# Graph attention: fetch each edge's row once in the maxima walk, store the rows in edge order, load them plainly in the sums walk, and weigh them on GpSimd

## The chip, the cores and the metric

One core of a Trainium2 chip runs a four-layer network (three graph layers of different kinds, and feed-forward parts between them) as one program. The metric is the device time of one execution in microseconds, the median of several. Engines are named as in the profile: PE (matrix), DVE (vector), ACT (scalar), POOL (GpSimd), SP (the engine that here only issues transfers).

## The reference, cut to what matters

Only the graph attention of the second layer is touched. It has 3125 nodes with 256 features (4 heads of 64) and 53125 edges, sorted by destination.

```
h = (x @ W).reshape(N, H, C)
a_s = jnp.einsum('nhc,hc->nh', h, att_src)
a_d = jnp.einsum('nhc,hc->nh', h, att_dst)
e = a_s[src] + a_d[dst]
e = jnp.where(e > 0, e, NEG_SLOPE * e)
m = jax.ops.segment_max(e, dst, num_segments=N)
p = jnp.exp(e - m[dst])
denom = jax.ops.segment_sum(p, dst, num_segments=N)
alpha = p / (denom[dst] + 1e-16)
msg = h[src] * alpha[:, :, None]
agg = jax.ops.segment_sum(msg, dst, num_segments=N)
```

The kernel first finds each destination's greatest `a_s` over its edges (the leaky step is monotonic, so the greatest `e` follows from it), and then sums weighted rows and weights, and divides at the end.

## The kernel before, in words

`graph_attention` (line 1495) has these stages in a row, each ended by a barrier of all engines.

**Rows and scores** (lines 1505 to 1580). PE makes `h` for 25 tiles of 128 nodes. Each row of 256 features and its 4 source scores goes to a table in DRAM, `table_gat` (rows of 260 floats), by one store per tile (line 1527). At the end the 4 source scores alone go to a second table, `table_max` (rows of 4 floats), by one store (line 1529).

**The maxima walk** (lines 1583 to 1690). The edges lie in 440 columns of 128 slots, taken in 110 quads of Q = 4 columns. Nothing here is scheduled by a planner: `written_out` writes out, for each engine, the steps of a turn in the order in which they are listed, each so many quads ahead. For each column POOL issues one gather of 128 rows (line 1625) from `table_max` into a ring of 8 quads; ACT makes diagonal matrices of three heads (line 1606) and a mask (line 1609), DVE those of the first head (line 1662) and the one-hot matrix of destinations (helper at line 126), PE spreads the scores over destinations (lines 1642 and 1644), and DVE takes the maxima (line 1673) and keeps them (line 1684).

**The sums walk** (lines 1693 to 1845), over the same 110 quads. POOL gathers 440 times 128 rows of 260 floats from `table_gat` (line 1737) into a ring of 8 quads in the tile `wide`. PE turns the one-hot matrix (line 1751), fetches each edge's destination scores by it (line 1760), and multiplies the one-hot matrix by the weighted rows (line 1768) into four banks, one for each column of a quad. ACT copies the turned matrix (line 1717) and takes the exponential (line 1722). DVE's turn for quad j is, in this order: one-hot of j+4 (line 126), weights times rows of j+1 (line 1828, 128x1024) with a copy of the weights behind them (line 1829), and then by turns the four additions of bank s to the node sums (line 1839) and the four small steps of the exponent of j+2 (lines 1809, 1812, 1816, 1821):

```
            mixed = [f for n in range(4) for f in ((0, add(n)), (2, exponents(n)))]
            written_out(R, (4, hots), (1, weigh), *mixed)
```

PE's turn is `(2, scores), (0, sums), (4, turn_hots)`. The product of bank s for the next quad waits until bank s has been added (`pe.wait_ge(added, j * Q + s + 1)`), an addition waits for the one before it, and a gather into a ring place waits until the sums of eight quads before are done. POOL has nothing but gathers in both walks; SP has one transfer at the start of the sums walk (line 1710, the nodes' own rows). Between that transfer and the walk DVE weighs the nodes' own rows (line 1792).

Of the kernel before, what the change touches and what calls it, by code (L numbers as in the profile page):

```python
# [16 lines left out]
ALU = mybir.AluOpType  # L17
# [161 lines left out]
def setup_memory(nc, ctx):  # L179
    class M:  # L180
        pass

    m = M()

    def sb(name, shape, dt=F32):
        return ctx.enter_context(nc.sbuf_tensor(name, shape, dt))

    m.X = sb("residual", [P, NT, D])
    m.XN = sb("normed", [P, NT, D])
    m.XT = sb("normed_T", [P, KD, NP])  # L190
    m.AGG = sb("sums", [P, NT, AW])
    m.BB = sb("wide", [P, 2 * NT * D])
    m.WS = sb("work", [P, 7168])
    m.PS = ctx.enter_context(nc.psum_tensor("ps", [P, 8, 512], F32))
    m.ident = sb("ident", [P, P])
    m.identb = sb("identb", [P, P], BF16)
    m.iota = sb("iota", [P, P])
    m.upto = sb("upto", [P, P])
    m.before = sb("before", [P, P])
    m.binsel = sb("binsel", [P, 2 * NT - 1], BF16)  # L200
    m.x_loaded, m.rec_blanked, m.rows_blanked = (
        nc.alloc_semaphore(s) for s in ("x_loaded", "rec_blanked", "rows_blanked"))
    m.ones = sb("ones", [P, P])
    m.zerob = sb("zerob", [P, 160], BF16)
    m.real = sb("real", [P, NT])
    m.wiota = sb("wiota", [NT, WP])
    m.coef = sb("coef", [P, KD, 2])
    m.gate = sb("gate", [P, NT, 8])

    m.lo1 = sb("lo1", [P, WP])  # L210
    m.src1 = sb("src1", [P, WP], I32)
    m.rel1 = sb("rel1", [P, WP], I32)
    m.tn1 = sb("tn1", [1, WP], I32)
    m.tn2 = sb("tn2", [1, WP], I32)
    m.lo_e, m.oth_e = sb("lo_e", [P, ET]), sb("oth_e", [P, ET])
    edges = m.XN[:].rearrange("p t d -> p (t d)")
    m.slot, m.type_e, m.col_e, m.row_e, m.lo_d, m.oth_d = (edges[:, k * ET:(k + 1) * ET] for k in range(6))
    m.record = sb("record", [P, ET], I32)
    m.forth, m.back = sb("forth", [P, 2, NT], I32), sb("back", [P, 2, NT], I32)
    m.expert = sb("expert", [1, 64], I32)  # L220
    m.onesb = sb("onesb", [P, P], BF16)
    m.notafterb = sb("notafterb", [P, P], BF16)
    m.beforeb = sb("beforeb", [P, P], BF16)
    m.iotah = sb("iotah", [P, WP], F16)
    m.zerow = sb("zerow", [P, WP + 1], BF16)
    m.AF = m.AGG[:].rearrange("p t d -> p (t d)")
    m.keys = [edges[:, k * ET:(k + 1) * ET].bitcast(I32) for k in range(6, 9)]
    m.keys_loaded = nc.alloc_semaphore("keys_loaded")
    m.blank = view(m.WS, 4352, BLANK // 4, EA + 4)
    m.zeros = view(m.WS, 5632, 6 * D)  # L230
    m.rec2 = nc.dram_tensor("rec2", (P * WP, EA + 4), F32).ap()
    m.rows_in = nc.dram_tensor("rows_in", (ROWS + 2 * P, D), F32).ap()
    m.rows_out = nc.dram_tensor("rows_out", (ROWS, D), F32).ap()
    m.table = nc.dram_tensor("table", (NP, D), F32).ap()
    m.table_gat = nc.dram_tensor("table_gat", (NP, D + 4), F32).ap()
    m.table_max = nc.dram_tensor("table_max", (NP, 4), F32).ap()
    m.table_rel = nc.dram_tensor("table_rel", (8 * NP, D), F32).ap()
    return m

# [1255 lines left out]
def graph_attention(nc, m, a):  # L1495
# [7 lines left out]


    with Stage(nc) as st:
        (loaded, made, copied, weighed, scored, rowed, bulked, tabled) = (
            st.sem(s) for s in ("loaded", "made", "copied", "weighed", "scored", "rowed", "bulked", "tabled"))
        stored = st.sems("stored", U)
        BANKS = 8
        row = view(m.WS, 0, U, RW)  # L1510
# [8 lines left out]
        def _(sp):  # L1519
# [5 lines left out]
            for t in range(NT):  # L1525
                sp.wait_ge(rowed, t + 1)
                sp.dma_start(to[:, t, :], row[:, t % U, :]).then_inc(stored[t % U], 16)
            sp.wait_ge(bulked, 1)
            sp.dma_start(m.table_max.rearrange("(t p) c -> p t c", p=P), src_score).then_inc(tabled, 16)
            for s in range(U):  # L1530
                sp.wait_ge(stored[s], 16 * (NT // U))
            sp.wait_ge(tabled, 16)

        @block.scalar
        def _(act):
# [24 lines left out]
        def _(dve):  # L1560
# [16 lines left out]
                             ).then_inc(scored, 1)  # L1577
            dve.wait_ge(scored, NT)
            v.tensor_copy(node[:, :, 0:H], scores[:, :, H:2 * H])
            v.tensor_copy(src_score, scores[:, :, 0:H]).then_inc(bulked, 1)  # L1580


    with Stage(nc) as st:
        names = ("hot", "masked", "made", "topped", "bested", "initial")
        hot, masked, made, topped, bested, initial = (st.sem(s) for s in names)
        R, RS = 8, 4
        gathered = st.sems("gathered", R * Q)
        S = view(m.WS, 0, RS * Q, P)
        off = view(m.WS, RS * Q * P, RS * Q * P // 2).bitcast(BF16).rearrange("p (u e) -> p u e", e=P)
        o = RS * Q * P * 3 // 2  # L1590
        rows = view(m.WS, o, R * Q, H)
        top = view(m.WS, o + R * Q * (H + 1), 2 * Q, H)
        minus = m.WS[:, o + R * Q * (2 * H + 1):o + R * Q * (2 * H + 1) + 1]
        diag = high[:, 0:RS * Q * H * P].rearrange("p (u h e) -> p u h e", u=RS * Q, h=H)
        MASK = float(2.0 ** 100)
        block = st.block()

        @block.scalar
        def _(act):
            def masks(j, u, r):  # L1600
                k = u % RS
                act.wait_ge(made, j + 1 + R - RS)
                for s in range(Q):
                    act.wait_ge(gathered[u * Q + s], r * 16 + 16)
                    for h in range(1, H):
                        nc.scalar.mul(diag[:, k * Q + s, h, :], m.ident[:], rows[:, u * Q + s, h:h + 1])  # L1606
                act.wait_ge(hot, j + 1)

                nc.scalar.activation(off[:, k * Q:(k + 1) * Q, :], S[:, k * Q:(k + 1) * Q, :], ACT.Identity,  # L1609
                                     bias=minus, scale=MASK).then_inc(masked, 1)  # L1610

            act.wait_ge(initial, 2)
            written_out(R, (2, masks))

        @block.gpsimd
        def _(pool):
# [1 line left out]
            nc.gpsimd.tensor_copy(best, src_score).then_inc(initial, 1)  # L1618

            def gather(j, u, r):  # L1620
                if j >= R:
                    pool.wait_ge(made, j + 1)
                for s in range(Q):
                    q, w = u * Q + s, j * Q + s
                    nc.gpsimd.indirect_dma_start(rows[:, q, :], None, m.table_max,  # L1625
                                                 bass.IndirectOffsetOnAxis(ap=m.src1[:, w:w + 1], axis=0)
                                                 ).then_inc(gathered[q], 16)

# [22 lines left out]
        def _(dve):  # L1651
# [3 lines left out]
            dve.wait_ge(initial, 2)  # L1655

            def first_heads(j, u, r):
                k = slice(u % RS * Q, (u % RS + 1) * Q)
                dve.wait_ge(made, j + 1 + R - RS)
                for s in range(Q):  # L1660
                    dve.wait_ge(gathered[u * Q + s], r * 16 + 16)
                v.tensor_tensor(diag[:, k, 0, :], m.ident[:].unsqueeze(1).to_broadcast([P, Q, P]),
                                rows[:, u * Q:(u + 1) * Q, 0:1].to_broadcast([P, Q, P]), ALU.mult)

            def hots(j, u, r):
                k = slice(u % RS * Q, (u % RS + 1) * Q)
# [26 lines left out]
    with Stage(nc) as st:  # L1693
# [2 lines left out]
        (dstep, ready, own_diffed, own_expd, selfed, hot, turned, tcopied, scored, taken, estep, diffed,  # L1696
         expd, weighted, summed, added) = (st.sem(s) for s in names)
        R, RT = 8, 4
        gathered = st.sems("gathered", R * Q)
        S = view(m.WS, 0, R * Q, P)  # L1700
        ST = view(m.WS, R * Q * P, RT * Q, P)
        o = (R + RT) * Q * P
# [5 lines left out]
        @block.sync  # L1708
        def _(sp):
            sp.dma_start(m.AGG[:, :, 0:RW], m.table_gat.rearrange("(t p) c -> p t c", p=P)).then_inc(selfed, 16)  # L1710

        @block.scalar
        def _(act):
# [15 lines left out]

        @block.gpsimd  # L1730
        def _(pool):
            def gather(j, u, r):
                if j >= R:
                    pool.wait_ge(summed, (j + 1) * Q)
                for s in range(Q):
                    q, w = u * Q + s, j * Q + s
                    nc.gpsimd.indirect_dma_start(rows[:, q, :], None, m.table_gat,  # L1737
                                                 bass.IndirectOffsetOnAxis(ap=m.src1[:, w:w + 1], axis=0)
                                                 ).then_inc(gathered[q], 16)

            written_out(R, (0, gather))

        @block.tensor
        def _(pe):
# [32 lines left out]
        def _(dve):  # L1777
# [22 lines left out]
            def exponents(n):  # L1800

                def step(j, u, r):
                    k = slice(u * Q, (u + 1) * Q)
                    sc = m.PS[:, 2 + u % 2, 0:Q * 8].rearrange("p (s c) -> p s c", s=Q)
                    if n == 0:
                        for s in range(Q):
                            dve.wait_ge(gathered[u * Q + s], r * 16 + 16)
                        dve.wait_ge(scored, j + 1)
                        v.tensor_tensor(e[:, k], rows[:, k, D:RW], sc[:, :, 0:H], ALU.add).then_inc(estep, 1)
                    if n == 1:  # L1810
# [10 lines left out]
                        v.tensor_scalar(e[:, k], e[:, k], 0.0, None, ALU.min).then_inc(diffed, 1)  # L1821
                return step

            def weigh(j, u, r):
                k = slice(u * Q, (u + 1) * Q)
                dve.wait_ge(expd, j + 1)
                f = rows[:, k, 0:D].rearrange("p s (h c) -> p s h c", h=H)
                v.tensor_tensor(f, f, p[:, k].unsqueeze(3).to_broadcast([P, Q, H, C]), ALU.mult)
                v.tensor_copy(rows[:, k, D:RW], p[:, k]).then_inc(weighted, 1)

            def add(s):

                def step(j, u, r):
# [8 lines left out]

            node_tile, tiles = NodeTiles(nc, dve, m.tn1), [None] * Q
            mixed = [f for n in range(4) for f in ((0, add(n)), (2, exponents(n)))]
            written_out(R, (4, hots), (1, weigh), *mixed)


    with Stage(nc) as st:
# [1318 lines left out]
```

## Time and profile before

| | us |
|---|---|
| median of three runs | 6393.75 |
| the three runs | 6400.41, 6391.69, 6393.75 |
| span of the profiled execution | 6396.8 |
| busy: PE, DVE, POOL, ACT | 4980.4, 3277.9, 3406.6, 1623.8 |

The profile gives no time for the profiled execution beside its span. Its span stands 3.05 us above the median of the runs. Busy shares are averages over some forty stages with different limits, so the two walks are read by themselves, from the lines, waits and timeline of their stretches. In a row of the timeline the first number is the start, the second the duration of that instruction or of a merged run of equal ones (`x4`); two instructions of one engine overlap by a little where they are pipelined.

### The profile page before, as it was taken

The numbers are of one execution on the slowest core, as the hardware profiler recorded it, in microseconds if no ns is written. First come the engines' busy times: TensorE is split into PE (matmuls) and PEld (weight loads), VectorE is DVE, ScalarE is ACT, GpSimd is POOL, SyncE is SP. The second block draws the span as 40 slices with busy tenths as digits, with TensorE's granted clock in tenths as the row PEclk, the third lists the DMA queues.
The fourth block names the chain that finished last, engine by engine and source line by source line (L and its number), as shares of the span: only waits on it lengthen the run. The fifth ranks groups of instructions, "written<-read, shape, count | busy, mean of one in ns | idle before, by whom it ended". The sixth has DMA issues, their size and how long they took to land. (4 is left out here: it accounts for less than half of the span.)

```text
span 6396.8 us, 72731 instructions
## 1 busy us (share of the span) xinstructions
PE 4980.4 (78%) x20184; PEld 3081.3 (48%) x20185; DVE 3277.9 (51%) x7777; ACT 1623.8 (25%) x3879; POOL 3406.6 (53%) x3602
## 2 busy tenths in 40 slices
PE   7968877887676888788863997799988568888455
PEld 2233334333445333355652886688875333343244
DVE  8954444444456777776772112566656332444412
ACT  4920002000323888511111221233331111000111
POOL 3147774777151777777735655467730211777223
PEclk7979998999788999888876998899999779999777
DMA  5023342334111000233323774333330334333255
GB/s 198 5 77 104 103 100 74 104 103 102 29 34 25 2 2 2 58 97 97 97 46 120 226 218 150 95 114 115 114 73 2 114 102 135 103 104 103 38 177 175
DMA packets 405943, 597.93 MB, mean 93 GB/s; under 512 B 131551, under 2 KB 305952, under 8 KB 405472
## 3 DMA queue, kind: packets, MB, share of 16 engines
q0 software_dynamic: 144992, 337.62, 20.1%
q1 hardware_dynamic: 257392, 252.99, 12.9%
q8 instruction: 151, 2.47, 0.2%
q10 hardware_dynamic: 3216, 3.28, 0.2%
q14 instruction: 192, 1.57, 0.1%
HBM read 472.47 MB, written 121.17 MB: 93 GB/s over the span
## 5 line engine op out<-in xcount | busy, mean ns | idle before, releaser
L784 PE MATMUL ps<-wide 128*128 128x256 f32 x2640 | 915.5, 429 | 323.0 <-DMA wide<-table,src 188.6
L811 DVE TENSOR_TENSOR sums<-sums,ps 128x256 f32 x1320 | 555.2, 421 | 981.8 <-PE ps L784 979.0
L769 POOL DMA_INDIRECT wide<-table,src x880 | 852.6, 969 | 276.5 <-PE ps L784 203.2
L784 PEld LDWEIGHTS ps<-wide 128*128 128x128 f32 x2640 | 407.3, 190 | 844.3 <-DMA wide<-table,src 557.6
L781 PE MATMUL ps<-zerow,zerob 128*128 128x440 bf16 x2640 | 713.4, 352 | 28.2 <-DVE wide L126 28.2
L769 POOL DMA_INDIRECT wide<-table_rel,rel x440 | 428.7, 974 | 351.5 <-ACTq L95 217.8
L1737 POOL DMA_INDIRECT wide<-table_gat,src x440 | 477.0, 1084 | 148.1 <-issue 122.8
L2379 POOL DMA_INDIRECT work<-table,work x440 | 451.8, 1027 | 187.8 <-issue 107.2
L1625 POOL DMA_INDIRECT work<-table_max,src x440 | 452.4, 1028 | 134.3 <-issue 134.3
L1644 PE MATMUL ps<-wide,work 128*128 128x512 f32 x880 | 451.1, 594 | 0.0
L1606 ACT ACTIVATE wide<-ident,work 128x128 f32<-128x128 f32 x1320 | 416.2, 388 | 64.9 <-DMA work<-table_max,src 61.1
L1768 PE MATMUL ps<-wide,work 128*128 128x260 f32 x880 | 332.3, 507 | 92.3 <-DVE sums L1839 92.0
L781 PEld LDWEIGHTS ps<-zerow,zerob 128*128 128x128 bf16 x2640 | 260.1, 99 | 223.5 <-DVE wide L126 29.9
L554 POOL DMA_INDIRECT rec<-sums,record x256 | 248.6, 971 | 176.0 <-DMA sums<-in_edge_attr 101.7
L719 ACT COPY work<-sums 128x256 f32<-128x256 f32 x100 | 33.1, 402 | 1203.1 <-PEq L723 1202.7
L1768 PEld LDWEIGHTS ps<-wide,work 128*128 128x128 f32 x880 | 178.4, 233 | 191.8 <-DVE sums L1839 162.9
L1673 DVE TENSOR_REDUCE work<-ps 128x16 f32<-128x2048 f32 x110 | 251.6, 2288 | 30.1 <-issue 27.3
L1642 PE MATMUL ps<-identb,work 128*128 128x512 bf16 x440 | 168.4, 383 | 125.9 <-ACT work L1609 125.9
L2407 PE MATMUL ps<-wide 128*128 x880 | 263.3, 381 | 1.1 <-DVE work L2445 1.1
L2408 PE MATMUL ps<-work,wide 128*128 128x256 f32 x880 | 262.7, 380 | 0.0
L701 PE MATMUL ps<-ident,normed 128*128 128x128 f32 x400 | 95.4, 425 | 199.7 <-DVE normed L647 199.3
L462 ACT ACTIVATE wide<-iotah,wide 128x441 f16<-128x441 f16 x416 | 230.3, 679 | 34.0 <-DVE wide L483 34.0
(474 smaller groups left out, 9031.7 us busy)
## 6 DMA issues: line engine op xcount, KB each, us to landing
wide<-in_L_ffn_W SPq DMA_DIRECT2D x64, 1024.0 KB, 6.0
wide<-in_L_ffn_expert_w SPq DMA_DIRECT2D x90, 256.0 KB, 3.2
table_rel<-wide SPq DMA_DIRECT2D x20, 1024.0 KB, 4.4
work<-rows_in SPq DMA_DIRECT2D x62, 256.0 KB, 5.7
rows_out<-work SPq DMA_DIRECT2D x62, 256.0 KB, 3.5
work<-rec SPq DMA_DIRECT2D x110, 136.0 KB, 2.2
rec<-work SPq DMA_DIRECT2D x27, 544.0 KB, 16.5
wide<-table,src POOLq DMA_INDIRECT x880, 2.8
```

The lines of the kernel that those rows point to most:

```text
L769: nc.gpsimd.indirect_dma_start(rows[:, w % RT, :], None, table, bass.IndirectOffsetOnAxis(ap=index[:, w:w + 1], axis=0)).then_inc(gathered ...
L781: nc.tensor.matmul(m.PS[:, w % (2 * Q), 0:WT], m.zerob[:, 0:P], m.zerow[:, 0:WT], start=True, stop=True)
L784: nc.tensor.matmul(m.PS[:, w % (2 * Q), 0:D], S[:, w % RT, :], rows[:, w % RT, :], start=True, stop=True).then_inc(summed, 1)
L811: v.tensor_tensor(at, at, m.PS[:, s, 0:D], ALU.add).then_inc(added, 1)
L1606: nc.scalar.mul(diag[:, k * Q + s, h, :], m.ident[:], rows[:, u * Q + s, h:h + 1])
L1625: nc.gpsimd.indirect_dma_start(rows[:, q, :], None, m.table_max, bass.IndirectOffsetOnAxis(ap=m.src1[:, w:w + 1], axis=0)).then_inc(gather ...
L1644: mm = nc.tensor.matmul(at, S[:, k * Q + s, :], diag[:, k * Q + s].rearrange("p h e -> p (h e)"), start=False, stop=True)
L1737: nc.gpsimd.indirect_dma_start(rows[:, q, :], None, m.table_gat, bass.IndirectOffsetOnAxis(ap=m.src1[:, w:w + 1], axis=0)).then_inc(gather ...
L1768: te.matmul(m.PS[:, 4 + s, 0:RW], S[:, u * Q + s, :], rows[:, u * Q + s, :], start=True, stop=True).then_inc(summed, 1)
L2379: nc.gpsimd.indirect_dma_start(rows[:, k, 0:D], None, m.table, bass.IndirectOffsetOnAxis(ap=idx[:, u * Q + s:u * Q + s + 1], axis=0)).then ...
L2407: te.matmul(at, ST[:, k, :], tile_at(by_src, tiles[s]), start=True, stop=False)
L2408: mm = te.matmul(at, attT[:, k, :], wa, start=False, stop=True)
```

## The change

The maxima walk now gathers whole rows of 260 floats from `table_gat` instead of rows of 4 floats from `table_max`, into a ring of 6 quads in the tile `sums` (which is free there). SP stores each quad of rows, in the order of the edges, to a new array `edge_rows` in DRAM (110 stores of 128x1040 floats, 520 KB each, one piece of 4160 bytes per partition). A gather into a ring place now also waits for the store that read it. `table_max` and its store are gone. In the sums walk SP loads the quads from `edge_rows` (110 loads of 520 KB) where POOL gathered, with the same wait on `summed`, and the multiplication of rows by weights with its copy moves from DVE to POOL, word for word. Other steps keep their order. The diff, cut to its core:

```diff
-    m.table_max = nc.dram_tensor("table_max", (NP, 4), F32).ap()
+    m.edge_rows = nc.dram_tensor("edge_rows", (P * WT, D + 4), F32).ap()
...
-            sp.wait_ge(bulked, 1)
-            sp.dma_start(m.table_max.rearrange("(t p) c -> p t c", p=P), src_score).then_inc(tabled, 16)
             for s in range(U):
                 sp.wait_ge(stored[s], 16 * (NT // U))
-            sp.wait_ge(tabled, 16)
...
-        R, RS = 8, 4
-        gathered = st.sems("gathered", R * Q)
+        R, RS, RR = 8, 4, 6
+        gathered, stored = st.sems("gathered", RR * Q), st.sems("stored", RR)
...
-        rows = view(m.WS, o, R * Q, H)
+        rows = view(m.AF, 0, RR * Q, RW)
...
+        @block.sync
+        def _(sp):
+            to = m.edge_rows.rearrange("(p w) c -> p w c", p=P)
+
+            def store(j, u, r):
+                g, n = j % RR, j // RR
+                for s in range(Q):
+                    sp.wait_ge(gathered[g * Q + s], n * 16 + 16)
+                sp.dma_start(to[:, j * Q:(j + 1) * Q, :], rows[:, g * Q:(g + 1) * Q, :]).then_inc(stored[g], 16)
+
+            written_out(R, (0, store))
+            for g in range(RR):
+                sp.wait_ge(stored[g], 16 * len(range(g, QUADS, RR)))
...
             def gather(j, u, r):
-                if j >= R:
-                    pool.wait_ge(made, j + 1)
+                if j >= RR:
+                    pool.wait_ge(made, j + 1 + R - RR)
+                    pool.wait_ge(stored[j % RR], j // RR * 16)
                 for s in range(Q):
-                    q, w = u * Q + s, j * Q + s
-                    nc.gpsimd.indirect_dma_start(rows[:, q, :], None, m.table_max,
+                    q, w = j % RR * Q + s, j * Q + s
+                    nc.gpsimd.indirect_dma_start(rows[:, q, :], None, m.table_gat,
                                                  bass.IndirectOffsetOnAxis(ap=m.src1[:, w:w + 1], axis=0)
                                                  ).then_inc(gathered[q], 16)
...
             sp.dma_start(m.AGG[:, :, 0:RW], m.table_gat.rearrange("(t p) c -> p t c", p=P)).then_inc(selfed, 16)
+            held = m.edge_rows.rearrange("(p w) c -> p w c", p=P)
+
+            def load(j, u, r):
+                if j >= R:
+                    sp.wait_ge(summed, (j + 1) * Q)
+                sp.dma_start(rows[:, u * Q:(u + 1) * Q, :], held[:, j * Q:(j + 1) * Q, :]).then_inc(came[u], 16)
+
+            written_out(R, (0, load))
...
         def _(pool):
-            def gather(j, u, r):
...
-            written_out(R, (0, gather))
+            g = nc.gpsimd
+
+            def weigh(j, u, r):
+                k = slice(u * Q, (u + 1) * Q)
+                pool.wait_ge(expd, j + 1)
+                f = rows[:, k, 0:D].rearrange("p s (h c) -> p s h c", h=H)
+                g.tensor_tensor(f, f, p[:, k].unsqueeze(3).to_broadcast([P, Q, H, C]), ALU.mult)
+                g.tensor_copy(rows[:, k, D:RW], p[:, k]).then_inc(weighted, 1)
+
+            written_out(R, (1, weigh))
...
-            def weigh(j, u, r):
-                k = slice(u * Q, (u + 1) * Q)
-                dve.wait_ge(expd, j + 1)
-                f = rows[:, k, 0:D].rearrange("p s (h c) -> p s h c", h=H)
-                v.tensor_tensor(f, f, p[:, k].unsqueeze(3).to_broadcast([P, Q, H, C]), ALU.mult)
-                v.tensor_copy(rows[:, k, D:RW], p[:, k]).then_inc(weighted, 1)
-
...
-            written_out(R, (4, hots), (1, weigh), *mixed)
+            written_out(R, (4, hots), *mixed)
```

DVE's queue in the middle of the sums walk, before: a turn from the one-hot matrix (L126) on. The weighing and its copy stand second and third; each `ISA` row is a wait ahead of an addition.

```order
L126 TENSOR_TENSOR work<-iota,lo 128x512 [waits sent2_4]
L1828 TENSOR_TENSOR wide<-wide,work 128x4x256 [waits split_2]
L1829 COPY wide<-work 128x4x4
L1839 ISA [waits sent3_4,sent2_4]
L1839 TENSOR_TENSOR sums<-sums,ps 128x260
L1809 TENSOR_TENSOR work<-wide,ps 128x16 [waits gathered23_24,gathered22_24,based_2,gathered31_23,gathered30_23]
L1839 ISA [waits sent3_4,sent2_4]
L1839 TENSOR_TENSOR sums<-sums,ps 128x260
L1812 SCALAR_TENSOR_TENSOR work<-work 128x16 [waits read_2]
```

The same turn now (L1851, L1828 and L1831 are the addition and the first two exponent steps by the new numbers). The addition comes straight behind the one-hot matrix, every second turn behind the load of node-tile numbers (L174), and the first exponent step waits for one load instead of four gathers.

```order
L126 TENSOR_TENSOR work<-iota,lo 128x512 [waits sent2_4]
L174 TENSOR_LOAD tn
L1851 ISA [waits sent3_4,sent2_4]
L1851 TENSOR_TENSOR sums<-sums,ps 128x260
L1828 TENSOR_TENSOR work<-wide,ps 128x16 [waits based_2,gathered13_8]
L1851 ISA [waits sent3_4,sent2_4]
L1851 TENSOR_TENSOR sums<-sums,ps 128x260
L1831 SCALAR_TENSOR_TENSOR work<-work 128x16 [waits read_2]
```

POOL's queue in the sums walk, before (the gathers, with a wait ahead of every fourth once the ring is full) and now (the weighing of each quad and its copy):

```order
L1737 DMA wide<-table_gat,src 128x260 x32
L1737 DMA wide<-table_gat,src 128x260 [waits sent2_4]
L1737 DMA wide<-table_gat,src 128x260 x3
L1737 DMA wide<-table_gat,src 128x260 [waits sent2_4]
L1737 DMA wide<-table_gat,src 128x260 x3
```

```order
L1750 UNCONDITIONAL_BRANCH [waits barrier_Pool_Activation_PE_DVE_SP_gather]
L1758 TENSOR_TENSOR wide<-wide,work 128x4x256 [waits split_2]
L1759 COPY wide<-work 128x4x4
L1758 TENSOR_TENSOR wide<-wide,work 128x4x256 [waits split_2]
L1759 COPY wide<-work 128x4x4
```

POOL's 440 gathers of this walk are gone, and 220 instructions on `wide` stand in their place, with one wait for each quad.

## Rows read from the trace of the kernel before

**Rows 1.** Lines of 2040 to 2655 us, the maxima walk: busy us, mean ns, idle before.

```profile
L1625 POOL DMA_INDIRECT work<-table_max,src x440 | 452.4, 1028 | 134.3 <-issue 134.3
L1606 ACT ACTIVATE wide<-ident,work 128x128 f32<-128x128 f32 x1320 | 416.2, 388 | 64.9 <-DMA work<-table_max,src 61.1
```

**Rows 2.** Lines of 2655 to 3300 us, the sums walk.

```profile
L1737 POOL DMA_INDIRECT wide<-table_gat,src x440 | 477.0, 1084 | 148.1 <-issue 122.8 <-SPq L95 14.3 <-PE ps L1768 11.0
...
L1839 DVE TENSOR_TENSOR sums<-sums,ps 128x260 f32 x440 | 186.4, 424 | 39.4 <-PE ps L1768 3.4 <-issue 2.2 <-DVE sums L1839 1.1
...
L1828 DVE TENSOR_TENSOR wide<-wide,work 128x1024 f32<-128x1024 f32 x110 | 134.2, 1220 | 0.9 <-ACT work L1722 0.8
```

**Rows 3.** Waits of 2700 to 3270 us: engine, line, waited for, us, times, longest.

```profile
DVE work L1809 <- DMA wide<-table_gat,src: 123.7, 80, 3.4
```

**Rows 4.** Timeline: first exponent step and last addition of the sums walk.

```profile
2683.55 0.17 DVE L1809 TENSOR_TENSOR work<-wide,ps 128x16 f32<-128x16 f32 x1 [2.76 <-PE ps L1760]
...
3281.28 0.42 DVE L1839 TENSOR_TENSOR sums<-sums,ps 128x260 f32 x1 [0.27 <-PE ps L1768]
```

**Rows 5.** Timeline of 2708 to 2722 us: DVE's turns and one turn of PE.

```profile
2709.24 0.69 DVE L126 TENSOR_TENSOR work<-iota,lo 128x512 f32<-128x512 f32 x1
...
2709.84 1.22 DVE L1828 TENSOR_TENSOR wide<-wide,work 128x1024 f32<-128x1024 f32 x1
...
2711.05 0.42 DVE L1839 TENSOR_TENSOR sums<-sums,ps 128x260 f32 x1
...
2711.94 2.21 PE L1768 MATMUL ps<-wide,work 128*128 128x260 f32 x8
2712.02 0.17 DVE L1812 SCALAR_TENSOR_TENSOR work<-work 128x16 f32<-128x16 f32 x1
...
2714.12 0.66 PE L1751 MATMUL ps<-ident,work 128*128 128x128 f32 x4
...
2714.61 0.96 PE L1760 MATMUL ps<-wide,work 128*128 x8
...
2721.65 0.68 DVE L126 TENSOR_TENSOR work<-iota,lo 128x512 f32<-128x512 f32 x1
```

**Rows 6.** Timeline: DVE and POOL instructions that run at the same time.

```profile
2671.62 6.83 DVE L1792 TENSOR_TENSOR sums<-sums,work 128x6400 f32<-128x6400 f32 x1 [0.35 <-ACT work L1727]
2672.81 6.47 POOL L1737 DMA_INDIRECT wide<-table_gat,src  x1 [0.30 <-issue]
...
3261.17 0.95 POOL L1737 DMA_INDIRECT wide<-table_gat,src  x1 [0.30 <-issue]
...
3261.75 0.37 DVE L1821 TENSOR_SCALAR work<-work 128x16 f32<-128x16 f32 x1
```

**Rows 7.** Lines of POOL over the whole program: its elementwise instructions.

```profile
L2677 POOL COPY work<-wide 128x128 f32 x56 | 16.6, 296 | 75.5 <-PE ps L2698 68.8 <-issue 5.7 <-POOL work L2677 1.0
L1053 POOL COPY sums<-normed 128x256 f32<-128x256 f32 x25 | 10.1, 402 | 75.7 <-DVE normed L1090 75.7
...
L2238 POOL TENSOR_SCALAR normed<-normed,work 128x256 f32<-128x256 f32 x11 | 6.0, 566 | 113.9 <-DVE work L2257 113.9
```

**Rows 8.** Timeline of SP around the end of the rows-and-scores stage.

```profile
2040.83 3.73 SPq L1527 DMA_DIRECT2D table_gat<-work  x4
2044.61 0.43 SPq L1529 DMA_DIRECT2D table_max<-wide  x1
```

**Rows 9.** DMA issues by line: KB each, median us from issue to landing.

```profile
wide<-in_L_ffn_W SPq DMA_DIRECT2D x64, 1024.0 KB, 6.0
...
work<-table_max,src POOLq DMA_INDIRECT x440, 2.4
wide<-table_gat,src POOLq DMA_INDIRECT x440, 2.8
...
table<-normed SPq DMA_DIRECT2D x10, 640.0 KB, 3.3
...
table_gat<-work SPq DMA_DIRECT2D x25, 130.0 KB, 2.1
...
table_max<-wide SPq DMA_DIRECT2D x1, 50.0 KB, 8.3
```

**Rows 10.** Stretches: busy of PE, PEld, DVE, ACT, POOL; granted clock, DMA share, GB/s.

```profile
2700.00:3270.00 570.00, 474.12 (x2082) 338.35 (x2080) 399.89 (x1148) 83.02 (x208) 441.29 (x410) 0.83 0.38 97
2704.00:2732.00 28.00, 26.26 (x137) 16.90 (x135) 25.15 (x72) 5.32 (x14) 21.91 (x21) 1.00 0.36 98
```

More of the change, by code:

```diff
@@ L1505, in graph_attention @@
     with Stage(nc) as st:
-        (loaded, made, copied, weighed, scored, rowed, bulked, tabled) = (
-            st.sem(s) for s in ("loaded", "made", "copied", "weighed", "scored", "rowed", "bulked", "tabled"))
+        (loaded, made, copied, weighed, scored, rowed) = (
+            st.sem(s) for s in ("loaded", "made", "copied", "weighed", "scored", "rowed"))
         stored = st.sems("stored", U)
@@ L1579, in _ @@
             v.tensor_copy(node[:, :, 0:H], scores[:, :, H:2 * H])
-            v.tensor_copy(src_score, scores[:, :, 0:H]).then_inc(bulked, 1)
+            v.tensor_copy(src_score, scores[:, :, 0:H])
     with Stage(nc) as st:
@@ L1590, in graph_attention @@
         o = RS * Q * P * 3 // 2
-        rows = view(m.WS, o, R * Q, H)
-        top = view(m.WS, o + R * Q * (H + 1), 2 * Q, H)
-        minus = m.WS[:, o + R * Q * (2 * H + 1):o + R * Q * (2 * H + 1) + 1]
+        top = view(m.WS, o, 2 * Q, H)
+        minus = m.WS[:, o + 2 * Q * H:o + 2 * Q * H + 1]
+        rows = view(m.AF, 0, RR * Q, RW)
         diag = high[:, 0:RS * Q * H * P].rearrange("p (u h e) -> p u h e", u=RS * Q, h=H)
@@ L1600, in masks @@
             def masks(j, u, r):
-                k = u % RS
+                k, g, n = u % RS, j % RR, j // RR
                 act.wait_ge(made, j + 1 + R - RS)
                 for s in range(Q):
-                    act.wait_ge(gathered[u * Q + s], r * 16 + 16)
+                    act.wait_ge(gathered[g * Q + s], n * 16 + 16)
                     for h in range(1, H):
-                        nc.scalar.mul(diag[:, k * Q + s, h, :], m.ident[:], rows[:, u * Q + s, h:h + 1])
+                        nc.scalar.mul(diag[:, k * Q + s, h, :], m.ident[:], rows[:, g * Q + s, D + h:D + h + 1])
                 act.wait_ge(hot, j + 1)
@@ L1657, in first_heads @@
             def first_heads(j, u, r):
-                k = slice(u % RS * Q, (u % RS + 1) * Q)
+                k, g, n = slice(u % RS * Q, (u % RS + 1) * Q), j % RR, j // RR
                 dve.wait_ge(made, j + 1 + R - RS)
                 for s in range(Q):
-                    dve.wait_ge(gathered[u * Q + s], r * 16 + 16)
+                    dve.wait_ge(gathered[g * Q + s], n * 16 + 16)
                 v.tensor_tensor(diag[:, k, 0, :], m.ident[:].unsqueeze(1).to_broadcast([P, Q, P]),
-                                rows[:, u * Q:(u + 1) * Q, 0:1].to_broadcast([P, Q, P]), ALU.mult)
+                                rows[:, g * Q:(g + 1) * Q, D:D + 1].to_broadcast([P, Q, P]), ALU.mult)
             def hots(j, u, r):
@@ L1698, in graph_attention @@
         R, RT = 8, 4
-        gathered = st.sems("gathered", R * Q)
+        came = st.sems("came", R)
         S = view(m.WS, 0, R * Q, P)
@@ L1731, in _ @@
         def _(pool):
-            def gather(j, u, r):
[L1733 to L1739, printed above, removed]
-            written_out(R, (0, gather))
+            g = nc.gpsimd
[6 more added lines that the diff above has]
+            written_out(R, (1, weigh))
         @block.tensor
@@ L1805, in step @@
                     if n == 0:
-                        for s in range(Q):
-                            dve.wait_ge(gathered[u * Q + s], r * 16 + 16)
+                        dve.wait_ge(came[u], r * 16 + 16)
                         dve.wait_ge(scored, j + 1)
```

## The prediction
> **What bounds the kernel now.** I read the profile in four steps. First the lines of the maxima walk, for an engine whose busy and idle times fill the stretch without a wait for anyone. POOL is that engine: 440 gathers take 452.4 us, and the 134.3 us between them are all "issue", its own cost of issuing [rows 1]. Together 586.7 us, 5.33 us for a quad of four. ACT, the next, has 416.2 us of diagonals and waits for gathers [rows 1].
>
> Then the lines of the sums walk. The gathers are again back to back, 477.0 + 148.1 = 625.1 us with a start of 14.3 [rows 2], and DVE's first exponent step waits 123.7 us for them in 80 of the turns [rows 3]. From the first exponent step at 2683.55 to the end of the last addition at 3281.70 the walk takes 598.2 us [rows 4], **5.44 us a quad**.
>
> Third, the timeline of the first turns, where the ring is still full of early gathers and no one waits for POOL: three turns of DVE, from the one-hot instruction at 2709.24 to that at 2721.65, take 12.41 us, **4.14 us a quad** [rows 5]. That is what DVE alone needs with the weighing on it. PE's turn there is 0.49 us for turning, 1.14 until the sums begin, and at most 2.21 for the sums, some 3.4 to 3.8 us [rows 5].
>
> Fourth, instructions of DVE and POOL that run at once. A gather that starts at 2672.81 under DVE's product of two SBUF tiles lasts 6.47 us instead of 0.95 and ends 0.8 us after that product [rows 6]: POOL could not go on beside it. The other direction shows once: a small DVE step that takes 0.17 elsewhere takes 0.37 under a gather [rows 6].
>
> **The change part by part.**
>
> *The table of maxima is not stored.* The stage ends when its last store has landed. That of the maxima is issued at 2044.61 and takes 8.3, to 2052.9; the last store of rows is issued by 2044.56 and takes 2.1, to 2046.7 [rows 8, 9]. Saved: **6 us**.
>
> *The maxima walk gathers rows 65 times as long.* What POOL spends on a gather hardly depends on the length of the row: 1028 against 1084 ns on average, and the second has the 6.47 us stall in it [rows 1, 2]. Landing goes from 2.4 to 2.8 us [rows 9], 0.4 us once, at the start. The ring of 6 quads covers 32 us of issue at 5.33. A place is used again after its row has landed (3), ACT has made its diagonals and PE its product (two turns more, some 11), and its store has landed: 520 KB lies between 130 and 640 KB, so 2.1 to 3.3 us [rows 9]. Both fit, so the new wait of the gathers costs nothing; if each of 110 waits took 0.05 us of POOL's time it would be 5 us. The DMA engines are 0.38 busy with such gathers [rows 10]; a store every 5.33 us, even at its full 3.3, would bring them to about 1.0, at (3.3 - 2.1) x 390 / 510 = 0.9 us of pure moving to 0.55. I take the second, as a landing time is mostly fixed. The new tail is hidden: the last store lands some 6 us after the last gather is issued, and PE and DVE work on for longer. In sum 0 us, bounds 0 and +15.
>
> *The sums walk loads.* A load of 520 KB takes less than the 6.0 us of 1024 KB [rows 9], is issued seven quads ahead, and waits on SP, where nothing else is queued. So the 123.7 us of waits for gathers go [rows 3]. SP's first load stands behind the nodes' own rows, but the walk starts only when DVE has weighed those, so the start stays.
>
> *The weighing moves from DVE to POOL.* DVE's turn loses 2711.05 - 2709.84 = 1.21 us [rows 5]: 4.14 - 1.21 = **2.93 us**. POOL gets an instruction W of 128x1024 and a small copy. No row has a POOL instruction on two tiles. A copy costs 296 ns at 128 and 402 at 256 elements, that is 0.83 ns for an element and 190 fixed; the tensor_scalar of 256 takes 566, so 1.47 ns for an element [rows 7]. Lower bound for W: two operands at the copy's pace, 2 x 0.83 x 1024 + 190 = 1.9 us. Upper: twice the tensor_scalar's, 3.2 us. I take the tensor_scalar's pace plus one more operand at the copy's, 2.30 x 1024 + 190 = **2.5 us**, as the tensor_scalar is the nearest instruction.
>
> Does W lie beside DVE's work? The weights of quad j+2 are ready when DVE's turn ends, and DVE starts the next one-hot instruction at once, a product of two SBUF tiles of 0.69 us. By the stall of 6.47 us POOL waits for it [rows 6]. Then W starts, and I take it that DVE's instructions with two SBUF inputs in turn wait for W. The additions and the first exponent step read one side from PSUM and go on; the second exponent step (line 1812) reads two SBUF operands and stands 0.97 us after the first addition [rows 5], so 0.60 + 0.97 = 1.57 us into the turn. W ends at 0.69 + 2.5 = 3.2. DVE loses 1.65 us, and the turn is 2.93 + 1.65 = **4.6 us**. In general the turn is W + 2.05. PE needs 3.4 to 3.8 and follows; its clock, 0.83 over the walk, was 1.00 where turns took 4.14 [rows 10]. The node-tile loads that lose their cover under the weighing lie in DVE's new wait. The copy behind W (0.2 us) I count as going after DVE's step; if it goes first the turn is 4.8 and 22 us are lost.
>
> The Trainium skill (SBUF — State Buffer, "Who interferes with whom") says that DVE and GpSimd share one pair of ports under an exclusive lock held for a whole instruction, and that a DVE instruction with two SBUF inputs contends with a GpSimd one that reads SBUF. By that rule, which speaks against this change, the turn is the 4.6 above; without it, the 3.6 of the first rival. The 6.47 us agree for one direction. The page GPSIMD Engine Reference ("Elementwise — side-by-side cycle accounting") has 4497 ns for a two-input addition of 2048 elements, by which I estimate W at 2.3 us; the turn would be 4.4 and the time 22 us lower. No run here shows it yet.
>
> **Sum.** Sums walk: 110 x (5.44 - 4.6) = 92 us saved, 1 us lost on the first W, which is longer than DVE's was. With 6 from the table: 97 us. The profiled span of 6396.8 becomes 6300; the runs' median is 3.05 lower, and 6393.75 - 97 = **6297 us**. At W = 1.9 the turn is 3.95 and the time 6225; at 3.2 it is 5.25 and 6368.
>
> **The rivals.**
>
> *POOL and DVE do not block each other for whole instructions.* Then DVE's turn is 2.93 and PE's is the bound, 3.4 to 3.8; at 3.6 the walk saves 202 us, and the time is 6393.75 - 208 = 6186, up to 6212 at 3.84. For it: the single DVE stall under a gather is just 0.2 us. Against: the 6.47.
>
> *The maxima walk pays.* If stores and gathers delay each other, POOL's waits for stores appear. Four-fifths of the gain stays; at 15 us lost the time is 6312.
>
> *Slower: W is longer than 3.45 us.* POOL's weights are one value repeated 64 times in a pattern of four dimensions, and no POOL row has such an operand. From W = 3.45 the turn passes 5.5 and the 6 us of the table are used up. At 4.0 the turn is 6.05, the walk 67 us longer, and the time 6393.75 + 67 - 5 = 6456. Against it: 4.0 us would be 3.7 ns for an element, 2.5 times the tensor_scalar's.
>
> **How the numbers follow.** Less than 0.2% (13 us) cannot be told from no change. Forecast with W between 2.1 and 3.1: 0.55. No blocking: 0.22. Maxima walk pays: 0.05, still faster. W of 3.1 to 3.3, within 13 us or a little faster: 0.07, of which 0.03 the same. Slower: 0.08. Something else, faster: 0.03. Faster 0.89, the same 0.03, slower 0.08. The range from 6195 to 6360 holds all of the forecast, half of the first rival (its upper part) and the second rival.
>
> **What would show it.** The maxima walk at 5.3 us a quad with POOL's gathers back to back and stores never waited for. In the sums walk no wait for DMA; W at 2.5 us starting as the one-hot instruction ends; the second exponent step (now line 1831) stretched from 0.17 to about 1.7 us, or idle as long before it. If that step keeps 0.17 us, the first rival holds. PE's clock near 1.00. The prediction is wrong if W is far from 2.5, or if PE, not DVE, has no idle time left.

## The result, and the profile after

The changed kernel takes a median of **6174.51 us** (6164.82 to 6176.51, 4 runs), the kernel before 6397.08 us (6391.69 to 6404.34, 4 runs) beside it. The ratio is 0.9649, 95% interval 0.9637 to 0.9661: faster by 3.5%, 222.6 us. The forecast of 6297 us had the sign and missed the size: 97 us were expected, and the time lies below the range, whose low end was 6195.

The profiled spans are 6396.8 and 6172.5 us, 224.3 apart. In pieces, each from two marks that both traces have:

| piece | before, us | after, us | gained, us |
|---|---|---|---|
| end of the rows-and-scores stage: last DVE copy to first gather | 10.28 | 3.65 | 6.6 |
| maxima walk: first gather to SP's load of the nodes' own rows | 599.9 | 606.2 | -6.3 |
| from that load to the first exponent step | 29.04 | 25.20 | 3.8 |
| sums walk: first exponent step to end of the last addition | 598.2 | 383.9 | 214.3 |
| the rest of the program, whose code is unchanged | | | 5.9 |

The last line is the difference of two executions, 3.2 us ahead of the first mark and 2.7 behind the last. So nearly all of the gain is the sums walk, 3.49 us a quad in place of 5.44. Its two marks in the timeline after, against [rows 4] (columns: start, duration, engine and line, idle time before):

```profile
2676.23 0.17 DVE L1828 TENSOR_TENSOR work<-wide,ps 128x16 f32<-128x16 f32 x1 [2.73 <-PE ps L1780]
...
3059.66 0.43 DVE L1851 TENSOR_TENSOR sums<-sums,ps 128x260 f32 x1 [0.21 <-DVE sums L1851]
```

The lines of the sums walk after (2640 to 3070 us), against [rows 2]:

```profile
L1788 PE MATMUL ps<-wide,work 128*128 128x260 f32 x880 | 223.8, 398 | 13.1 <-POOL wide L1759 13.1
L1758 POOL TENSOR_TENSOR wide<-wide,work 128x1024 f32<-128x1024 f32 x110 | 222.4, 2021 | 189.3 <-ACT work L1742 189.3
L1851 DVE TENSOR_TENSOR sums<-sums,ps 128x260 f32 x440 | 185.5, 422 | 35.5 <-PE ps L1788 6.6 <-DVE sums L1851 1.1
...
L1831 DVE SCALAR_TENSOR_TENSOR work<-work 128x16 f32<-128x16 f32 x110 | 94.7, 860 | 0.1
...
L1835 DVE TENSOR_TENSOR work<-work,ps 128x16 f32<-128x16 f32 x110 | 17.4, 158 | 0.1
```

POOL has no gathers here any more, and no engine waits for a DMA. L1758 is W, the product of rows and weights: 2.02 us. L1831 is the second exponent step: of the same shape as the third (L1835, 158 ns), it takes 860, with no idle time charged to it. And POOL waits 189.3 us for ACT, and even PE waits 13.1 us for POOL. This looks like a ring, in which each engine waits for another, and the waits over 2700 to 3040 us (engine and line, waited for, us, times, longest) show the links that cross engines:

```profile
ACT work L1742 <- DVE work L1840: 127.6, 98, 1.6
POOL wide L1758 <- ACT work L1742: 127.2, 99, 1.6
...
PE ps L1788 <- POOL wide L1759: 9.7, 49, 0.4
```

One whole turn, from one one-hot instruction to the next, in the timeline:

```profile
2803.00 0.69 DVE L126 TENSOR_TENSOR work<-iota,lo 128x512 f32<-128x512 f32 x1
...
2803.42 2.03 POOL L1758 TENSOR_TENSOR wide<-wide,work 128x1024 f32<-128x1024 f32 x1 [1.28 <-ACT work L1742]
...
2804.57 0.90 DVE L1831 SCALAR_TENSOR_TENSOR work<-work 128x16 f32<-128x16 f32 x1
...
2805.40 0.19 POOL L1759 COPY wide<-work 128x16 f32<-128x16 f32 x1
2805.40 0.41 DVE L1851 TENSOR_TENSOR sums<-sums,ps 128x260 f32 x1
...
2806.45 0.69 DVE L126 TENSOR_TENSOR work<-iota,lo 128x512 f32<-128x512 f32 x1
```

The turn is 3.45 us. W runs from 0.42 to 2.45 us into it, the second step begins at 1.57 and is done 0.02 after W, and then DVE needs 1.00 us to the next one-hot instruction. The ring is: DVE's last step gives ACT the scores, ACT's exponential starts W, W holds DVE's second step, and that holds the last step of the next quad.

The granted clock and the DMA share, against [rows 10] (stretch, its length, busy of PE, PEld, DVE, ACT, POOL, clock, DMA share, GB/s):

```profile
2690.00:3040.00 350.00, 339.25 (x2036) 293.15 (x2034) 321.60 (x914) 81.60 (x203) 220.26 (x204) 1.00 0.53 154
2620.00:2630.00 10.00, 7.31 (x21) 3.07 (x20) 4.81 (x8) 5.80 (x18) 7.75 (x8) 1.00 0.93 96
2040.00:2640.00 600.00, 492.86 (x1308) 201.75 (x1308) 435.31 (x759) 482.94 (x1427) 451.97 (x444) 0.98 0.66 196
```

PE is at its full clock over the sums walk, where it had 0.83. It is busy 97% of the stretch and has little slack, so this profile alone does not say whether the ring or PE sets the 3.45 us. That was the first question for the experiments.

### The profile page after: what moved, and what is told of

It is laid out like the page before. It is cut to its first block and busy times, and to the rows that moved or that the text cites. A ratio compares the mean times of both kernels' runs of the same rounds, so it can differ in the third digit from the quotient of the medians.

```text
span 6172.5 us, 72727 instructions
## 1 busy us (share of the span) xinstructions
PE 4857.4 (79%) x20184; PEld 3040.4 (49%) x20185; DVE 3202.2 (52%) x7557; ACT 1622.2 (26%) x3879; POOL 3157.2 (51%) x3382
## 5 line engine op out<-in xcount | busy, mean ns | idle before, releaser
L1637 POOL DMA_INDIRECT sums<-table_gat,src x440 | 451.2, 1026 | 134.3 <-issue 134.3
L1617 ACT ACTIVATE wide<-ident,sums 128x128 f32<-128x128 f32 x1320 | 416.4, 388 | 82.5 <-DMA sums<-table_gat,src 79.2
L1758 POOL TENSOR_TENSOR wide<-wide,work 128x1024 f32<-128x1024 f32 x110 | 222.4, 2021 | 189.3 <-ACT work L1742 189.3
L1788 PE MATMUL ps<-wide,work 128*128 128x260 f32 x880 | 223.8, 398 | 13.1 <-POOL wide L1759 13.1
```

## The experiments

A walk's turn below is the time from its first exponent step to the end of its last addition, divided by 110 quads; a steady turn is one-hot to one-hot in the timeline. The runs below went to three chips, and gains are taken against the kernel before on the same chip: 6390.45 us beside the first four below, 6401.47 beside both at once, the longer ring, the maxima side and its tail, 6397.77 beside the other order and the best of both.

**The loads without the move.** The weighing and its small copy go back to DVE:

```diff
...
+            def weigh(j, u, r):
+                k = slice(u * Q, (u + 1) * Q)
+                dve.wait_ge(expd, j + 1)
+                f = rows[:, k, 0:D].rearrange("p s (h c) -> p s h c", h=H)
+                v.tensor_tensor(f, f, p[:, k].unsqueeze(3).to_broadcast([P, Q, H, C]), ALU.mult)
+                v.tensor_copy(rows[:, k, D:RW], p[:, k]).then_inc(weighted, 1)
...
-            written_out(R, (4, hots), *mixed)
+            written_out(R, (4, hots), (1, weigh), *mixed)
```

> The changed kernel with the weighing and its copy put back on DVE; the loads and stores stay. What the first turns of the kernel before showed (4.14 us a quad where no one waited for a gather) should now hold for the whole walk: the turn goes from 3.44 to 4.14, the time from 6174 to about 6251 us. If the loads themselves were slow or PE set the pace, it would stay nearer 6174. In either case no wait for a load.

Measured: 6248.12 us, ratio 0.9776 (0.9760 to 0.9792). The timeline has DVE's turn:

```profile
2802.55 0.68 DVE L126 TENSOR_TENSOR work<-iota,lo 128x512 f32<-128x512 f32 x1
...
2806.69 0.68 DVE L126 TENSOR_TENSOR work<-iota,lo 128x512 f32<-128x512 f32 x1
```

That is 4.14 us, as the turns of before had where they waited for no gather [rows 5]. The loads are worth 142 us of the 223, and moving the weighing, once they are there, the other 81.

**The move without the loads.** The kernel before, with only the weighing on POOL, behind the gathers of the quad six ahead:

```diff
+            def weigh(j, u, r):
+                k = slice(u * Q, (u + 1) * Q)
+                pool.wait_ge(expd, j + 1)
...
+                nc.gpsimd.tensor_tensor(f, f, p[:, k].unsqueeze(3).to_broadcast([P, Q, H, C]), ALU.mult)
+                nc.gpsimd.tensor_copy(rows[:, k, D:RW], p[:, k]).then_inc(weighted, 1)
...
+            written_out(R, (6, gather), (1, weigh))
...
```

> The kernel before with only the weighing moved to POOL; the gathers of the sums walk stay there. POOL is one queue: four gathers at 1.33 us and a product of about 2.0 with its copy of 0.2 make 7.5 us a quad against 5.44, so 6397 + 110 x 2.1 = about 6625. If POOL could build a gather's descriptors beside its product, it would stay near 6397.

Measured: 6573.66 us (one run), 183 us slower than before. The timeline:

```profile
2900.86 1.91 POOL L1745 TENSOR_TENSOR wide<-wide,work 128x1024 f32<-128x1024 f32 x1
...
2907.28 2.52 DVE L1828 TENSOR_SCALAR work<-work 128x16 f32<-128x16 f32 x1
2907.86 1.91 POOL L1745 TENSOR_TENSOR wide<-wide,work 128x1024 f32<-128x1024 f32 x1
2909.70 0.75 POOL L1746 COPY wide<-work 128x16 f32<-128x16 f32 x1
2909.72 0.68 DVE L126 TENSOR_TENSOR work<-iota,lo 128x512 f32<-128x512 f32 x1
```

The turn shown is 7.00 us (7.09 is the mean of the walk), POOL's own sum: four gathers of 1.25, W of 1.9 and the small copy. So neither part alone gives what both give; the first makes the room that the second uses. W takes 1.91 us where DVE's one-hot instruction is not beside it. The DVE step of 2.52 us is the last exponent step, 0.17 elsewhere. It has one SBUF input, and it ends with W, having begun under a gather. The forecast's turn had no such case, though the 0.37 us of [rows 6] are this same step. The Trainium skill (SBUF — State Buffer, "Who interferes with whom") has it: it lists tensor_scalar among the instructions that can enter a mode which takes the port pair shared with GpSimd. This run agrees. It shows the lock the other way round as well: the small copy on POOL, 0.20 us elsewhere, takes 0.75 beside DVE's one-hot instruction and ends with it.

**Less work for PE.** From the third quad on, three of the four transposes are left out, so the scores of three columns in four come from stale one-hot tiles:

```diff
-                for s in range(Q):
+                for s in range(Q if j < 2 else 1):
```

> The changed kernel with three of the four transposes of each quad left out in the sums walk (from the third quad on), so the destination scores of three columns in four are stale. PE's turn is then some 0.4 us shorter. PE theory: 0.4 x 110 = 44 us less, about 6130. Ring theory: the turn stays between 3.32 and 3.44, 0 to 13 us less, and PE waits for POOL's copy for the rest.

Measured: 6178.34 us (one run), the walk's turn 3.50 us. The line of the sums in this run:

```profile
L1788 PE MATMUL ps<-wide,work 128*128 128x260 f32 x880 | 225.8, 400 | 29.7 <-POOL wide L1759 29.7
```

PE was given less to do: it is busy 88% of the stretch from 2700 to 3040 us, and it waits 29.7 us for POOL in place of 13.1. The walk is no shorter, 3.50 us a turn against 3.49, so PE did not set the 3.45 us. The time is 212 us under the kernel before beside it, not more than the 223 of the kernel after.

**The second step's input from PSUM.** One more small DVE instruction writes the step's input e to a free piece of PSUM, and the second step reads one side there:

```diff
+                    held_e = m.PS[:, 2 + u % 2, 64:64 + Q * H].rearrange("p (s c) -> p s c", s=Q)
...
+                        v.tensor_tensor(held_e, rows[:, k, D:RW], sc[:, :, 0:H], ALU.add).then_inc(estep, 1)
...
-                        v.scalar_tensor_tensor(lk[:, k], e[:, k], 0.2, e[:, k], ALU.mult, ALU.max
+                        v.scalar_tensor_tensor(lk[:, k], held_e, 0.2, e[:, k], ALU.mult, ALU.max
```

> The changed kernel, with one operand of the second exponent step put in PSUM by one more small DVE instruction, so that the step reads a single SBUF operand. Ring theory (DVE's last exponent step, ACT's exponential, POOL's product, port free, DVE's second step, and round again sets the turn of 3.44 us): the step falls from 0.86 to 0.17 us, and the turn to what PE needs, about 3.25, some 20 us less, 6154. PE theory (PE has no idle time left, the blocked step only fills DVE's slack): the step falls to 0.17 as well, but the turn stays within 0.05 us, the time within 5 us of 6174. If the port is not the cause, the step stays at 0.86.

Measured: 6130.54 us, ratio 0.9591 (0.9575 to 0.9607). Lines of its sums walk:

```profile
L1758 POOL TENSOR_TENSOR wide<-wide,work 128x1024 f32<-128x1024 f32 x110 | 222.2, 2020 | 150.7 <-ACT work L1742 150.7
L1788 PE MATMUL ps<-wide,work 128*128 128x260 f32 x880 | 221.9, 395 | 1.7 <-POOL wide L1759 1.7
...
L1833 DVE SCALAR_TENSOR_TENSOR work<-ps,work 128x16 f32<-128x16 f32 x110 | 18.4, 167 | 0.1
```

The stretch of 2690 to 3010 us, with the columns of the windows above:

```profile
2690.00:3010.00 320.00, 320.00 (x2075) 290.66 (x2074) 278.44 (x1035) 83.18 (x207) 223.05 (x206) 1.00 0.54 171
```

The step takes 167 ns instead of 860, though W is as long as ever and runs beside it. The steady turn falls from 3.45 to 3.09 us and the walk's from 3.49 to 3.14, which is 38 us. PE now waits for POOL 1.7 us in all and is busy through the whole stretch: it is the bound. Its turn is 3.09 us, less than I gave it, so the gain is larger than expected.

**Both at once.** The two edits above together:

> The operand in PSUM and three of four transposes left out together (the latter as in the run before, so destination scores of three columns in four are stale). Ring theory: with both limits gone the turn falls to DVE's own, 2.93 us plus 0.1 to 0.25 for the loads of tile numbers, about 3.1, some 38 us under 6174. PE theory: no more than the transposes alone gave.

Measured: 6124.99 us (one run); the steady turn is 2.94 us:

```profile
2800.89 0.68 DVE L126 TENSOR_TENSOR work<-iota,lo 128x512 f32<-128x512 f32 x1
...
2802.47 0.17 DVE L1833 SCALAR_TENSOR_TENSOR work<-ps,work 128x16 f32<-128x16 f32 x1
...
2803.83 0.68 DVE L126 TENSOR_TENSOR work<-iota,lo 128x512 f32<-128x512 f32 x1
```

With ring and PE both relieved the turn is DVE's own, the 2.93 us of the prediction; the one small instruction more does not lengthen it. The 0.15 us under the turn of the run before are what PE alone had held. So less PE work is worth nothing while the ring stands, and 12 us of walk (345 to 333) once it is gone.

**A longer ring.** A copy of 128x128 on POOL ahead of each W, behind a wait for POOL's own small copy of the quad before:

```diff
+                if j:
+                    pool.wait_ge(weighted, j)
+                g.tensor_copy(spare, m.ones[:])
```

> The changed kernel with one more POOL copy of 128x128 (0.30 us) ahead of each product, inside the ring. Ring theory: the turn grows by about 0.3, the time by 33 us to 6207. PE theory: POOL idles 1.28 us in each turn, so 0 to 10 us.

Measured: 6209.55 us (one run); lines of its sums walk:

```profile
L1762 POOL TENSOR_TENSOR wide<-wide,work 128x1024 f32<-128x1024 f32 x110 | 209.0, 1900 | 0.0
...
L1835 DVE SCALAR_TENSOR_TENSOR work<-work 128x16 f32<-128x16 f32 x110 | 122.5, 1113 | 0.1
```

The second step grows by 0.25 us, from 0.86 to 1.11, and the walk's turn by 0.25 to 3.74, with PE and DVE given nothing more. The copy takes over the wait for the one-hot instruction that W had: its own record is 0.43 us, and W's is down to 1.90.

**Another order of DVE's turn.** The second step later, under less of W:

```diff
-            mixed = [f for n in range(4) for f in ((0, add(n)), (2, exponents(n)))]
+            mixed = [(0, add(0)), (2, exponents(0)), (0, add(1)), (0, add(2)), (2, exponents(1)), (0, add(3)),
+                     (2, exponents(2)), (2, exponents(3))]
```

> The changed kernel with the same instructions in another order in DVE's turn of the sums walk: addition 0, exponent step 0, additions 1 and 2, step 1, addition 3, steps 2 and 3. The step that reads two SBUF operands then comes about 2.3 us after the last step of the turn before, where POOL's product ends at 2.4, so it is hardly blocked. Ring theory: its duration falls from 0.86 to 0.2 to 0.4 us and the turn from 3.49 to about 3.3, some 20 us less than the changed kernel's 6174. If the length of the wait does not depend on the place in the turn, nothing changes.

Measured: 6164.29 us, ratio 0.9637 (0.9621 to 0.9653). Its second step:

```profile
L1831 DVE SCALAR_TENSOR_TENSOR work<-work 128x16 f32<-128x16 f32 x110 | 26.3, 239 | 0.1
```

The stretch is nearly gone, 239 ns, but the walk's turn is 3.42 us: steady turns alternate between 3.24 and 3.44. The remaining steps now stand at the end of the turn, one behind the other, and the additions wait for each other (23.8 us, 1.1 in the kernel after). By the ratios this is 8 us under the kernel after, of the 20 expected, and the two intervals overlap. A better place in the order does not do what another source for the operand does.

**The maxima side alone.** Rows gathered and stored as in the kernel after, the sums walk as in the kernel before (whose diff read backwards this is, from the sums walk on):

> The changed kernel up to the end of the maxima walk, with the sums walk of the kernel before (gathers on POOL, weighing on DVE). It shows what the maxima side alone costs: 6.6 us saved by the store of the small table, 6 to 8 us lost at the walk's end, where the last 12 columns are gathered later than before. Net 0 to +2 us against the kernel before; if the stores cost more in ways the single trace hides, +5 or more.

Measured: 6404.3 us against 6401.47, ratio 1.0013 (0.9987 to 1.0039): the 6 us saved ahead of the walk and its longer tail cancel.

**The tail of the maxima walk.** In the kernel after, 22.1 us pass from the last gather's issue to SP's load of the own rows, against 14.6 before. The last 12 columns hold only blanks, all with index 0, so that each of the 128 partitions reads the same row. The source view of those gathers, 2615 to 2630 us, and of the same stretch when the blank columns have the indices of a column 40 earlier (2623 to 2642 us of that run):

```profile
DMA to landing us min/median/max: 3.8/7.8/9.1
```

```profile
DMA to landing us min/median/max: 2.8/3.1/3.7
```

```diff
+            def near(w):
+                return w if w < 428 else w - 40
...
-                                                 bass.IndirectOffsetOnAxis(ap=m.src1[:, w:w + 1], axis=0)
+                                                 bass.IndirectOffsetOnAxis(ap=m.src1[:, near(w):near(w) + 1], axis=0)
```

> The changed kernel, with the gathers of columns 428 to 439, in which every slot is blank and names node 0, given the indices of 12 filled columns instead (their rows count for nothing either way). If the late landings at the end of the maxima walk (8 to 9 us instead of 2.9) come from 128 reads of one row, they fall to about 3 and the walk's end comes some 6 us earlier. If they come from the stores beside them, nothing changes.

Measured: 6172.23 us, ratio 0.9641 (0.9625 to 0.9657). The tail is 14.8 us, 7.3 less. The total cannot be told from the kernel after by its interval; only the trace shows the gain.

**The best of both.** The PSUM input and the blanks' indices together:

> The operand in PSUM and the indices of filled columns for the 12 blank ones together. The two act in different walks, so they add up: turn 3.14 us as in the run with the PSUM operand alone, the end of the maxima walk as in the run with the indices alone, some 40 + 4 us under the changed kernel, 6126.

Measured: 6129.25 us, ratio 0.9581 (0.9565 to 0.9597), 43 us under the kernel after by the ratios; the tail 14.8 and the walk's turn 3.14 us. It beats both kernels. Over the PSUM input alone it has the shorter tail in its trace and no gain in time beyond the intervals.

## Why the prediction was wrong in size

**The step that failed is "the turn is W + 2.05", 4.6 us.** It measured 3.45. The 1.15 us a quad times 110 are 126 us, and 6297 - 126 = 6171. That this comes so near to the 6174.51 is partly luck, as the smaller misses below (6.3 and some 4 us lost, 3.8, 0.6 and 5.9 gained) nearly cancel. The mechanism of the step held; three of its numbers did not:

- *W = 2.5 us.* Alone it takes 1.90 us (first product of the walk, the run with the longer ring). This is the lower bound of the prediction, two operands at the copy's pace. I took the tensor_scalar because it seemed the nearest instruction; that was the wrong neighbour, and it is 0.64 of the 1.15 (2.54 unrounded). The Trainium skill (GPSIMD Engine Reference, "Elementwise — side-by-side cycle accounting") gave an estimate of 2.3 us from its 4497 ns for 2048 elements, too long as well.
- *W starts when the one-hot instruction is done, at 0.69.* W's record starts at 0.42, right behind ACT, and is 0.13 us longer than W alone: by this it was held only until about 0.55, while DVE's next instruction starts at 0.60. This is 0.14 us. The run with the longer ring agrees: there the copy stands first and takes the 0.13, and W takes 1.90. A wait for the port is counted in the duration and not as idle time, on POOL here and on DVE in L1831.
- *After W comes the second step, and then the rest: 1.36 us.* Measured from W's end it is 1.00. The next addition starts at 2805.40, 0.05 before W's record ends, and the step behind which it stood is recorded as ending after it has begun. This is 0.36 us.

**The lock itself** is shown from both sides. Taking the second step's SBUF input away brings it to 167 ns and the turn to PE's bound; making PE's work less does nothing; making the ring longer by a POOL copy lengthens step and turn alike. The first rival (no blocking, PE the bound at 3.4 to 3.8 us) gave 6186 us, nearer to the result than the forecast, for the wrong reason: PE's own turn is 3.09 us, and the walk is not at it. That closeness is why a time alone would not have settled this.

**DVE's own turn of 2.93 us** was right: 2.94 with ring and PE both relieved. In the kernel after, the walk's first turns (up to 4.91 us) and a few later ones (3.57 to 3.79) lift the mean to 3.49; that is some 4 us which the sum does not have. **PE's turn** was put too long at 3.4 to 3.8; it was read where PE was still waiting for other engines. **The granted clock** was right, 1.00.

**The table of maxima**, 6 us forecast, gave 6.6.

**The maxima walk**, 0 us with bounds 0 and +15, cost 6.3. POOL stayed back to back (451.2 and 134.3 us, [rows 1]) and never waited for a store; the stores land in 3.1 us, within 2.1 to 3.3. The page's rows of the two issues:

```profile
edge_rows<-sums SPq DMA_DIRECT2D x110, 520.0 KB, 3.1
wide<-edge_rows SPq DMA_DIRECT2D x110, 520.0 KB, 3.6
```

What was missed is the tail of blank columns. Before, it existed too, in the last gathers of the sums walk: from 3255 us on they landed in 5.3 to 8.1 us, and the last three turns waited 3.4, 2.4 and 2.5 us for them. So a part of the tail was not new, and moved from one walk to the other. The DMA share was put at 0.55 and measured 0.66; it had no price, save in those last 10 us at 0.93.

**Loads without waits** was right, at a landing time of 3.6 us. **The start of the sums walk** was taken as unchanged; it gave 3.8 us, as the nodes' own rows no longer arrive beside POOL's first gathers: DVE waits 14.7, 13.9 and 13.9 us for them in the three traces that have these gathers (before, the move without the loads, the maxima side alone), and 10.9 to 11.2 in the nine that have loads.

**The small copy behind W** was right to be left out of the turn: at 2805.40 it runs beside an addition.

**The slower rival** (W over 3.45 us, 6456 us) fell with W. Its worry was the repeated weight in a pattern of four dimensions. At 1.90 us for 1024 elements W came out at the lower bound, which had been worked out for plain operands; no run has the product of plain operands beside it.

## What to carry to other kernels

Before moving a product of two SBUF tiles from DVE to POOL, list which DVE instructions of the turn read two SBUF operands, or may take the shared port with one, and when POOL's product runs against them. The turn is then a ring and not the longest engine, and it is shortened by taking one operand from PSUM, here 37 us for one more small instruction. A price bounded by two neighbours deserves a chance at each end: with W at 1.9 us the prediction's own formula gave 3.95 us a turn and 6225 us, more than half of the way from the forecast to the result, but the forecast's chance began at a W of 2.1. A queue that becomes free can be worth more than the work taken off it: without the gathers gone, the same move made the kernel 183 us slower.

## What was not expected of the hardware

- A POOL product of two SBUF operands over 128x1024 f32 takes 1.90 us, DVE's 1.22. If the copy's fixed 190 ns hold for it, it is 1.67 ns an element, twice the copy's 0.83.
- A DVE tensor_scalar of 16 elements with one SBUF input took 2.52 us under POOL's gather and product, where it takes 0.17 alone. The additions and the first exponent step, which read one side from PSUM, kept their 0.42 and 0.17 us under W.
- Gathers of one and the same row by all 128 partitions land in up to 9.1 us, against 2.9 at the median of the walk, and keep the DMA engines 0.93 busy at 96 GB/s. The replacement of their indices brings them to 3.1, so it is the repeated row and not the load of the stores.
- It is the product more than the gather that holds this step. In the move without the loads all 43 steps of 2.36 us or more began under a gather with W right behind it. With no product behind, in the three traces that have gathers in this walk, a step that began up to 0.51 us into a gather took 0.17 us, and one that began 0.53 us or later ended with the gather, at 0.42 us at most.
- Not tried: whether the ring would go with the one-hot instruction moved as well.
